# Splitting and re-dealing the products of a top-k FFN stage, two maxima per score tile, and straight-line, overlapped fronts in one Trainium2 kernel

## The reference

```python
# stage 0: long convolution, x1 = x2 = ctx, v = layernorm(x)
y = irfft(rfft(v * x2) * rfft(k))[..., :L] + (v * x2) * skip
x = x + tanh(g_xattn[0]) * einsum(y, x1)
# stage 4: attention with 32 heads in 8 groups
scores = q @ k.T / sqrt(hd); w = softmax(masked(scores)); out = w @ v
# stage 5: top-k FFN
z = layernorm(x) @ ternary(W_syn).T + b_syn          # 2048 columns
thresh = top_k(z, 204)[-1]
hidden = where(z >= thresh, relu(z), 0)
out = layernorm(h + hidden @ ternary(W_out).T + b_out) * gamma + beta
# stage 6: causal attention with rotary embedding, its weights as f16 pairs
```

## Time and profile before

| | us |
|---|---|
| median of three runs (3606.24 to 3606.59) | 3606.37 |
| the profiled execution | 3601.69 |
| its span in the profile | 3599.9 |
| busy in the span: PE, DVE, ACT, POOL | 2964.1, 2606.7, 1641.7, 872.3 |
| stage 0, up to the last convolution step | 0 to 420 |
| stage 4, first to last maximum | 1016 to 1438 |
| stage 5, products to the last scale | 1497 to 2175 |

### The profile page before, as it was taken

How to read it: one execution, slowest core, us unless ns; L and a number is a source line. 1 busy time by engine, 2 the same in 40 slices (tenths; PEclk the granted TensorE clock), 3 DMA queues, 4 the chain that set the end, 5 groups by cost and what they waited for, 6 DMA issues and landing times.

```text
span 3599.9 us, 50392 instructions
## 1 busy us (share of the span) xinstructions
PE 2964.1 (82%) x18610; PEld 1735.8 (48%) x18610; DVE 2606.7 (72%) x4530; ACT 1641.7 (46%) x2565; POOL 872.3 (24%) x1293
## 2 busy tenths in 40 slices
PE   3899899884668888578788745899999999998898
PEld 1343476663334444256566522444444444444565
DVE  4799769999756666588888874677777777776333
ACT  3000044444335555138778862444444444455343
POOL 2454200000000000015666682222222222221000
PEclk8899999997879999799989967999999999999999
DMA  7222022212211010200000021000000000012000
GB/s 263 83 79 76 27 59 71 59 48 71 54 24 30 22 24 10 97 30 2 1 1 2 4 87 53 7 7 1 7 7 1 7 7 1 7 37 61 13 17 17
DMA packets 52642, 132.51 MB, mean 37 GB/s; under 512 B 6416, under 2 KB 19536, under 8 KB 51152
## 3 DMA queue, kind: packets, MB, share of 16 engines
q1 hardware_dynamic: 43216, 96.11, 8.7%
q10 hardware_dynamic: 9216, 33.56, 3.1%
HBM read 119.03 MB, written 4.19 MB: 34 GB/s over the span
## 4 chain that ended last, share of the span: by engine, by line
PE 37%; DVE 17%; issue 10%; ACT 7%; POOL 1%; DMA 0%; DVEq 0%; SPq 0%; POOLq 0%; ACTq 0%
PE psum L1093 11%; PE psum L2392 3%; PE psum L1904 3%; PE psum L2433 3%; ACT area_g L1982 2%; PE psum L2417 2%; DVE area_c L2035 2%; PE psum L1918 2%; PE psum L1315 2%; PE psum L1334 2%; PE psum L2402 2%; DVE area_a L1651 2%; PE psum L1294 1%; PE psum L1939 1%; DVE small L2671 1%
## 5 line engine op out<-in xcount | busy, mean ns | idle before, releaser
L1982 ACT ACTIVATE area_g<-area_a 128x2048 bf16<-128x2048 f32 x156 | 310.6, 1995 | 43.7 <-DVE area_a L2053 30.2
L1904 PE MATMUL psum<-area_c,ident_bf 128*128 128x128 bf16 x3584 | 245.1, 232 | 100.3 <-DVE area_c L2035 100.3
L2671 DVE TENSOR_REDUCE small<-psum 128x1 f32<-128x384 f32 (+1 forms) x256 | 159.1, 622 | 188.5 <-PE psum L2393 188.5
L515 PE MATMUL psum<-area_b,area_g 128*128 128x512 f32 x640 | 281.2, 599 | 16.0 <-DVE area_g L464 14.4
L172 POOL TENSOR_TENSOR rstd<-mean_var,eps_col 128x2 f32<-128x2 f32 x65 | 16.3, 251 | 1139.9 <-DVE mean_var L581 528.4
L1904 PEld LDWEIGHTS psum<-area_c,ident_bf 128*128 128x128 bf16 x3584 | 227.8, 105 | 129.6 <-DVE area_c L2035 122.9
L659 PE MATMUL psum<-xT_high,area_a 128*128 128x256 f16 x1024 | 237.8, 280 | 1.4 <-DVE xT_low L596 1.4
L659 PE MATMUL psum<-xT_low,area_a 128*128 128x256 f16 x1024 | 237.4, 280 | 0.0
L2392 PE MATMUL psum<-area_b,stage 128*128 128x512 f32 (+1 forms) x512 | 234.5, 540 | 0.0
L2543 ACT ACTIVATE area_g<-psum 128x384 f16<-128x384 f32 (+1 forms) x256 | 139.3, 544 | 168.7 <-PE psum L2402 166.7
L515 PEld LDWEIGHTS psum<-area_b,area_g 128*128 128x128 f32 x640 | 121.3, 192 | 175.2 <-issue 164.6
(11 more groups left out here) (394 smaller groups left out, 7548.6 us busy)
## 6 DMA issues: line engine op xcount, KB each, us to landing
stage<-in_w ACTq DMA_DIRECT2D x24, 512.0 KB, 4.3
stage<-in_w SPq DMA_DIRECT2D x24, 512.0 KB, 3.7
area_g<-in_toeplitz SPq DMA_DIRECT2D x32, 256.0 KB, 3.5
area_b<-in_ctxT SPq DMA_DIRECT2D x16, 512.0 KB, 3.9
area_b<-area_b SPq DMA_DIRECT2D x24, 256.0 KB, 3.7
x_stream<-in_x SPq DMA_DIRECT2D x4, 1024.0 KB, 8.9
area_c<-in_ctxT SPq DMA_DIRECT2D x4, 1024.0 KB, 15.4
area_g<-in_ctx SPq DMA_DIRECT2D x8, 512.0 KB, 5.2
```

The costliest lines, as they stand in the source:

```text
L515: last = nc.tensor.matmul(psum[:, 4 * par + m, :], toep[:, par, (m - k) * P:(m - k + 1) * P], kv[:, par, k, :], start=(k == 0), stop=(k == m))
L1904: last = nc.tensor.matmul(psum[:, 1, t_ * P:(t_ + 1) * P], identb[:, :], above5[:, t_, c * P:(c + 1) * P], start=(c == 0), stop=(c == KE - 1))
L1982: nc.scalar.activation(junk5[t_], z5[b % 3][:, t_, :], ACT.Sign, bias=fine5[:, par, t_:t_ + 1], scale=-1.0, accum_out=signs5[:, t_:t_ + 1] ...
L2671: nc.vector.tensor_reduce(nmax6[:, n % 2:n % 2 + 1], psum[:, 2 + n % 2, 0:nk], AX.X, ALU.min).then_inc(sig("nmax6_ready"), 1)
```

## The change

Three places.

**Stage 0.** The front is written out over 8 batches instead of a loop, in another order: sums of batch b+1 are taken ahead of the copies of b, the scaling of b+1 ahead of the skip additions of b, and POOL makes the root of b+1 ahead of the skip products of b. The convolution's first two trips (LEAD0 = 2, four steps) now run before the preparation of stage 1's thresholds; PE waits for all their banks to be drained first. The chunks of stage 1's weights begin after those, so four of the 8 steps without a chunk stand first and four last.

**Stage 4.** One maximum of two banks becomes two of one bank each, and scores wait and signal by bank.

**Stage 5.** Synapse and output units are cut in halves of 4 matmuls and dealt over all steps by the tables below (number m is half m % 2 of unit m // 2). Before, synapse n stood whole in step n + 2, and the outputs were `{4: (0,), 6: (1,), 8: (2,), 9: (3,), 10: (4, 5), 11: (6,), 12: (7,)}`. With them move the drains, lows (one step later), maxima (steps 7 and 11, were 10 and 11), y's sums, scale and finish (up to one step into the next period), and chunks: four ternary chunks of W_out go from period 0 to period -1; all 16 splits of stage 6's weights stand in period 8, the first 8 in pairs in steps 1 to 4 (before: 12 in period 8, one per step, and 4 in period 9). POOL's finish of the last batch moves into stage 6, one tile behind the first key chunk and one behind the first query chunk.

```diff
-            for n, name in enumerate(("w0_up", "w0_gate", "w0_down", None)):
-                with dve.Fori(4 * n, 4 * n + 4) as i:
+            for first, trips, name in ((0, 2, None), (2, 4, "w0_up"), (6, 4, "w0_gate"), (10, 4, "w0_down"), (14, 2, None)):
+                if first == LEAD0:
+                    prep_dve(dve, dc, prep1, 1, None)
+                    nc.vector.tensor_copy(part[:, 30:31], gates[:, 0:1]).then_inc(sig("tables_ready"), 1)
+                with dve.Fori(first, first + trips) as i:
...
             def maxima(i, st, u):
-                dve.wait_ge(sig("s4_ready"), nth(i, st, G2, u + 1))
-                src = psum[:, 2:4, :].rearrange("p a (h k) -> p (a h) k", h=2)
-                nc.vector.tensor_reduce(max4[:, st % 2, 4 * u:4 * u + 4], src, AX.X, ALU.max, negate=True).then_inc(sig("max4_ready"), 1)
+                for n in range(2):
+                    dve.wait_ge(sig("s4_ready"), nth(i, st, 2 * G2, 2 * u + n + 1))
+                    src = psum[:, 2 + n, :].rearrange("p (h k) -> p h k", h=2)
+                    nc.vector.tensor_reduce(max4[:, st % 2, 4 * u + 2 * n:4 * u + 2 * n + 2], src, AX.X, ALU.max,
+                                            negate=True).then_inc(sig("max4_ready"), 1)
...
+        SYNAPSE5 = {0: (0, 1), 1: (2, 3), 2: (4, 5), 3: (6, 7), 4: (8, 9), 5: (10,), 6: (11,), 7: (12, 13), 8: (14,), 9: (15,)}
+        OUT5 = {4: (0,), 5: (1,), 6: (2,), 7: (3,), 8: (4,), 9: (5,), 10: (6, 7, 8), 11: (9, 10), 12: (11, 12), 13: (13, 14, 15)}
+        DRAIN5 = {1: 0, 2: 1, 3: 2, 4: 3, 5: 4, 7: 5, 8: 6, 10: 7}
...
+            CHUNKS5 = {1: (0, 1), 2: (2, 3), 3: (4, 5), 4: (6, 7), 5: (8,), 6: (9,), 7: (10,), 8: (11,), 10: (12,), 11: (13,), 12: (14,), 13: (15,)}
-                    if p == 0 and k < 8:
-                        ternary_chunk(dve, dc, prep5, 8 + k)
+                    if p == -1 and k in (4, 6, 8, 9):
+                        ternary_chunk(dve, dc, prep5, 8 + (4, 6, 8, 9).index(k))
+                    if p == 0 and k < 4:
+                        ternary_chunk(dve, dc, prep5, 12 + k)
...
-                    if live(p - 2) and k == 11:
-                        y_sum(p - 2, 0)
                     if live(p - 2) and k == 13:
-                        y_sum(p - 2, 1)
-                        y_scale(p - 2, 0)
+                        y_sum(p - 2, 0)
```

More of the change, by code:

```diff
@@ L439, in dve_stage0 @@
             dve.wait_ge(sig("x_loaded"), 64)
[L440 to L454, removed]
+            norm_sums(dve, dc, 0, 0)
@@ L1940, in out @@
                                                 stop=(k == KE - 1 and m == 1))
-                if c == 3:
+                if n % 4 == 3 and half:
                     last.then_inc(sig("y5_ready"), 1)
@@ L1958, in pe_stage5 @@
                             fold(p, k, t_)
-                    if live(p + 1) and 2 <= k < 10:
-                        synapse(p + 1, k - 2)
+                    if live(p + 1):
+                        for m in SYNAPSE5.get(k, ()):
+                            synapse(p + 1, m // 2, m % 2)
                     if live(p - 2) and 1 <= k < 9:
@@ L1963, in pe_stage5 @@
                     if live(p - 2):
-                        for n in outs.get(k, ()):
-                            out(p - 2, n)
+                        for m in OUT5.get(k, ()):
+                            out(p - 2, m // 2, m % 2)
                     if 1 <= p + 2 <= B and k in (11, 12):
@@ L2151, in dve_stage5 @@
                         x_stats(bx, xi)
-                    if live(p + 1) and 3 <= k < 11:
-                        drain(p + 1, k - 3)
-                    if live(p - 2) and 2 <= k < 10:
-                        low(p - 2, k - 2)
+                    if live(p - 2) and 3 <= k < 11:
+                        low(p - 2, k - 3)
+                    if live(p + 1) and k in DRAIN5:
+                        drain(p + 1, DRAIN5[k])
+                    if p == B:
+                        for n in CHUNKS5.get(k, ()):
+                            split_chunk(dve, dc, prep6, n)
+                    if p == B + 1 and k == 11:
+                        tables6(dve, dc)
                     if 1 <= bx <= B and k == 9:
                         x_scale(bx, xi)
-                    if live(p + 1) and k in (10, 11):
-                        maximum(p + 1, k - 10)
-                    if live(p - 2) and k == 11:
-                        y_sum(p - 2, 0)
+                    if live(p + 1) and k in (7, 11):
+                        maximum(p + 1, k // 11)
                     if 1 <= bx <= B and k in (12, 13):
```

185 lines of the change are left out of this document (106 added, 79 removed).

## The result

| | before | after |
|---|---|---|
| median, 20 runs each, us | 3606.26 | 3611.74 |
| lowest and highest | 3603.55, 3608.64 | 3605.03, 3616.88 |
| ratio, 95% interval | | 1.0015, 1.0008 to 1.0022 |
| profiled execution, its span | 3601.69, 3599.9 | 3614.04, 3612.2 |

The changed kernel is 0.15% slower by that ratio; I had forecast 1.3% faster, and no time of it falls into the range of 3542 to 3587 that I gave.

The account below looks back on a forecast made before the run. No engine alone bounds the kernel; PE's work is bunched against DVE's. Terms -14 - 12 - 15 - 5.5 - 1 = -47.5 took the profiled 3601.7 to 3554, from the median 3559 us; forecast 3548 to 3569, wider range 3542 to 3587.

Parts of the forecast that it names:

- the 68.7 of the sum: Stage 5, periods 2 to 6: forecast us per period, summed over its steps, where the five took 72.1 each.
- Stage 5, periods 2 to 6: Evened work of PE and DVE takes 3 us off each of five periods, -15.
- (a): Stage 5 period heads: clock stays low, +3.4 in 5 periods, 3576; chance 0.16, alone or with period 8's upper bound.
- (b): Stage 5, periods 2 to 6: low clock lasts into step 4, slower than before, +55, 3629; chance 0.07.
- the mixed case: Low clock at stage 5's period heads together with a load-bound stage 0 front, 3592 to 3604; chance 0.05.
- Stage 0: Front batches 9.2 us instead of 11.4 (-15.4), preparation moved (-2.7), interrupted pipeline (+4.5); about -14.
- Rival (c): Stage 0's front is bound by loads, 11.4 us a batch as before; stage gives +2, total 3575; chance 0.10.
- Stage 4: Maxima by bank: -8 at the start, -4 in the steady part; -12, bounds -3 and -16.
- The ends of stage 5: Periods -1 (+3), 0 (-4.5), 7 (-2), 8 (+5) and 9 (-7); sum -5.5.
- The -5 and +7: Stage 5, new deal of splits and chunks: period 8 loses 5 us, period 9 gains 7.
- Stage 6's entry: First key chunk no longer stands behind the last finishes on POOL, first query still behind one; -1.
- The rule weighed in the prediction: Stage 5, period 8: by the shared port lock every split pair blocks POOL outright, +10, total 3564.

Follow-up runs that it names:

- e2: The changed kernel with the turns of batch p-2 one step earlier on PE and the lows one step earlier on DVE; 3564.04 us, ratio 0.9890.
- e12: e2 with the splits dealt as in the kernel before, 12 in period 8 and 4 in period 9; ratio 0.9910, from three executions.
- e3: The changed kernel without its stage 5 and stage 6 parts; 3592.52 us, ratio 0.9969.
- e5: Only the stage 4 part of the change, on the kernel before; 3598.03 us, ratio 0.9984.
- e9: e2 with period 8's splits in other steps, one in each of steps 1 to 10, two in 11 to 13; 3565.70 us, ratio 0.9893.

## Why the prediction was wrong

- **Bound and reading of before:** right. DVE and PE bunched against each other, and the new deal does even them out: e2 has 69.0 and 69.1 for the 68.7 of the sum, at full clock.
- **Stage 5, periods 2 to 6 (-15, measured +30.5):** the step that failed is the one that made each step the larger of PE's work and DVE's work. That holds only while no instruction of a step waits for one that the other engine does late in the same step. I listed what stands in each step and never asked, for the moved drain, everything that it waits for: its second wait, on the turn of three batches back, stood in the code, two steps away before and none after. e1 puts the turn ahead of the synapse within the step and gets 7.5 us a period back, e2 restores one step of distance and gets 9.9.
- **The rivals:** the slower case I priced at 3629 was of another mechanism, the clock. The clock rose at the heads, as the forecast said, and (a) and (b) both fall. The mechanism that decided was missing among them. (The 0.89 for faster counts 0.01 of the mixed case of 0.05, not most of it.)
- **Stage 0 (-14, measured -6.3):** the front is as worked out, 9.2 us a batch:

```profile
43.75 1.28 DVE L586 BATCH_NORM_STATS2 stats<-x_stream 128x6 f32<-128x512 f32 x2
...
52.98 1.28 DVE L586 BATCH_NORM_STATS2 stats<-x_stream 128x6 f32<-128x512 f32 x2
```

  The first drain came 20.1 us earlier, 18.1 by my terms. The failed step is "the steps without a weight chunk are as many as before, only half of them come first": four of them cost 6.9 us more at the start, where PE has no stock. The interruption cost 5.7, 4.5 in the sum. The remaining 1.2 is spread over the other steps. Rival (c) falls.
- **Stage 4 (-12, measured -3.4):** the start gave 7.0 for the 8 I had. The steady -4 was wrong, it came as +3.6: shorter waits of the scores for maxima don't shorten sixteen groups at full clock, and three more short stretches at 1.2 GHz than before ate half of the start's gain (3.6 of 7.0). The standstill of PE is in both kernels and no part of this difference.
- **The ends of stage 5 (-5.5):** periods -1 and 0 together -4.7 (stage 4's last maximum to period 0's end; -1.5 predicted), period 7 0 for -2, periods 8 and 9 -4.8 for -2. Period 8 alone 69.8 for 64.6. Period 1, for which I had no change, +1.6. The -5 and +7 inside the last of these are shown by e12; the other ends were not tried by themselves. **Stage 6's entry** gave nothing, 0 for -1.
- In all, -47.5 was predicted and +12.4 came. Of the difference of 60 us, 45.5 are periods 2 to 6, 7.7 stage 0 and 8.6 stage 4; the ends gave 1.6 more than expected. The rule weighed in the prediction, on the port that VectorE and GpSimd share, would have had the total 5 us higher through period 8; the trace has 5.2 there, as I took it. The lock itself shows: "SBUF — State Buffer" of the Trainium skill, in the section "SBUF: two separate sides", has the one that comes second block for the whole instruction of the first, and the trace agrees (POOL's 1.88 us beside the splits, for a median of 0.31).

## What to carry to other kernels

When an instruction is moved to another step, list every semaphore it waits on, those for buffer reuse too, and for each the distance in steps to what raises it, before and after; a distance of zero chains two engines, and what stands ahead of the raiser in its queue is then in the chain. A schedule's sum of larger-of-two per step is worth writing down even so: once the distance was restored, its total was right within 0.5%, its single steps within 1.4 us. Work that is free at a pipeline's end, since there is stock to run down, isn't free at its start.

## What the runs showed of the hardware

The twenty executions of the changed kernel spread over 12 us and those of the kernel before over 5, without any change of the work. Part of this goes with the clock: the three fastest (3605.0 to 3607.1) had a mean grant of 0.946 over the whole execution, the four slowest (3614.5 to 3616.9) 0.943 to 0.944. In the steady part of stage 4 the grant fell to 1.2 GHz between 1 and 6 times in one profile for a short stretch, and sixteen groups took 54.5 us without and 1.6 us more for each. I had not expected a stage whose PE is busy for seven eighths of the time to lose its clock. One fall came at the same distance from the stage's first maximum in several kernels (233 us in e1, e2, e3, e5, e9 and e12), right behind the standstill of PE of some 3 us for which the profile names no releaser. What DVE pays for two reduces of 512 PSUM columns each in place of one of 1024 is 0.14 us: 2 x 0.68 against 1.22.
